# Order of the second layer's matmuls in two-tile expert blocks of an adaLN, attention and mixture-of-experts kernel

## The chip, the cores and the metric

The kernel runs on one core of a Trainium2 chip. The metric is the device time of one execution in microseconds (us), the median of the runs. TensorE is written PE (its weight loads PEld), VectorE is DVE, ScalarE is ACT, GpSimd is POOL, SyncE is SP.

## The reference

The input is 4096 tokens of 256 features. Two residual steps follow each other:

```
h = layernorm(x) * (1 + ca) + sa
x = x + ga * attention(h)          # 16 heads of 64, linear attention
h = layernorm(x) * (1 + cb) + sb
x = x + gb * ffn(h)

gate_probs = softmax(x @ Wg + bg)                 # 8 experts, the top 2 are kept and renormalised
h   = gelu(einsum('bsf,efh->bseh', x, W1) + b1)   # 256 -> 1024
out = einsum('bseh,ehf->bsef', h, W2) + b2        # 1024 -> 256
y   = einsum('bsef,bse->bsf', out, selected)
```

Only the second step's expert part is touched by the change. The kernel computes each token for its two chosen experts alone.

## The kernel before, in words

After attention and routing, the tokens of each expert stand in a list, and the rest of the kernel (from about 405 us of the trace) works through it in *blocks*. A block holds three tiles or two tiles of 128 tokens of one expert. Each expert first runs one or two three-tile blocks (`Fori(0, three)`, L1610) and then its two-tile blocks (`Fori(0, two)`, L1622); the counts come from the data. The experts run in a loop over three pairs, with the last pair written out behind it (`experts`, L391). Even and odd experts use two sets of weight buffers, and the next expert's weights are split in the last engines' spare time of a three-tile block.

fp32 precision is made of three matmuls: each operand is split into a high and a low part, and high*high, high*low, low*high are added (`three_terms`, L369). One block goes through the engines like this:

1. PE, `first` (L1572): 8 slices m of the hidden dimension, 6 matmuls each, 48 in all, into PSUM banks 0 to 3. It starts when DVE has written `xT_lo` (semaphore `s_blo`, L1575). After every second slice it adds one to `s_f1`.
2. ACT, `rows_block` (L811): for each pair of slices k = 0 to 3, waits for `s_f1`, applies the gelu twice into `hid` (L820), then copies the pair to `hid_hi` (L827).
3. DVE, `rows_block` (L1277): for each pair k, waits for ACT and writes `hid_lo` (L1289), which adds one to `s_hid`. Just ahead of pair 3 it does `take(gv + 1)` (L1251): it copies the next block's gate values and normalises the next block's three row tiles in `listed` (L1256, three instructions), which adds one to `s_norm`.
4. PE, `second` (L1591): out of `hid_hi`, `hid_lo` and the expert's `w2`, one accumulation per tile i, in bank 6 + i. It takes a range of slices (`chunks`); 3 matmuls per slice and tile, so 24 per tile and 48 per two-tile block. For tile 0 it waits for `s_hid` before each even slice (L1601); the other tiles use the same slices later and don't wait.
5. In the midst of `second`, PE runs `block_T(gv + 1)` (L1558): it waits for `s_norm` and transposes the next block's rows with 6 instructions (L1563).
6. ACT turns the transposed rows into `xT_full` (L801, two instructions), DVE splits them into `xT_hi` and `xT_lo` (L1247, L1248, two of each); the end of that allows the next block's `first`. POOL's `gather` (L567) also waits for the transposes: it then fetches the rows of the block after the next into `listed` by three indirect DMAs (L576).
7. When a tile's accumulation is complete (`s_f2`), DVE adds the bias and multiplies by the gate (L1299, L1300), and POOL scatters the tile to `out` with an accumulating indirect DMA (L588).

Each engine runs its own stream of instructions in the order in which they are written; semaphores alone tie them together. PE's stream in the two-tile loop is the only thing that the change touches. In the three-tile loop PE's order is: `most` (slices 0 to 5) of tile 0, the transposes, `most` of tile 1, `end` (slices 6 and 7) of tile 0, `most` of tile 2, `end` of tile 1, `end` of tile 2.

Of the kernel before, what the change touches and what calls it, by code (L numbers as in the profile page):

```python
# [26 lines left out]
M = FH // P  # L27
# [56 lines left out]
def adaln_block(nc, x, w_qkv, w_out, b_out, Wg, bg, W1, b1, W2, b2, cvec, wmod, out):  # L84
    ctx = ExitStack()
    with ctx:
# [282 lines left out]
        def three_terms(pairs):  # L369

            ops = [(a, b) for (ah, al), (bh, bl) in pairs for a, b in ((ah, bh), (ah, bl), (al, bh))]
            return [(a, b, i == 0, i == len(ops) - 1) for i, (a, b) in enumerate(ops)]
# [35 lines left out]
        def now(eng, reg):  # L408
            return eng.snap(reg, min_val=0, max_val=MAXB)
# [914 lines left out]
        def _(pe):  # L1324
# [233 lines left out]
            def block_T(n):  # L1558

                pe.wait_ge(s_norm, n + 1)  # L1560
                for c in range(C):
                    for i in range(BI):
                        last = pe.transpose(ps[:, XTB + c, i * P:(i + 1) * P], listed[:, i, c * P:(c + 1) * P], ident[:, :])  # L1563
                last.then_inc(s_bt, 1)
# [5 lines left out]
            def expert(e, par, three, two, last_expert):  # L1570

                def first(gv, size):  # L1572

                    T = size * P
                    pe.wait_ge(s_blo, gv + 1)  # L1575
                    for m in range(M):
                        k = m // 2
                        if m == 0:
                            pe.wait_ge(s_gelu, gv * 4 + FOUR)
                        if size == 3 and m in (4, 6):  # L1580
                            pe.wait_ge(s_gelu, gv * 4 + (k - 1 + FOUR))
                        if m == (3 if size == 3 else 6):
                            pe.wait_ge(s_y, gv * 3 + THREE)
                        to = ps[:, k, (m % 2) * T:(m % 2 + 1) * T] if size == 2 else ps[:, m % 4, 0:T]
                        col = slice(m * P, (m + 1) * P)
                        for w_, a, st, sp_ in three_terms([((w1_hi[par][:, c, col], w1_lo[par][:, c, col]), (xT_hi[:, c, 0:T], xT_lo[:, c, 0:T])) for c in range(C)]):
                            last = pe.matmul(to, w_, a, start=st, stop=sp_)  # L1587
                        if m % 2:
                            last.then_inc(s_f1, 1)

                def second(gv, size, i, chunks):  # L1591

                    bank = Y2 if i == 2 else Y0 + i
                    if 0 in chunks:
                        pe.wait_ge(s_y, gv * 3 + (i + 1))
                        if i == 2:
                            pe.wait_ge(s_gelu, gv * 4 + (M // 2 + FOUR))
                    r = slice(i * P, (i + 1) * P)
                    for m in chunks:
                        if i == 0 and m % 2 == 0:  # L1600
                            pe.wait_ge(s_hid, gv * 4 + (m // 2 + 1 + FOUR))  # L1601
                        for a, w_, st, sp_ in three_terms([((hid_hi[:, m, r], hid_lo[:, m, r]), (w2_hi[par][:, m, :], w2_lo[par][:, m, :]))]):
                            last = pe.matmul(ps[:, bank, 0:D], a, w_, start=m == 0 and st, stop=m == M - 1 and sp_)  # L1603
                    if M - 1 in chunks:
                        last.then_inc(s_f2, 1 if i < size - 1 else BI - i)

                pe.wait_ge(s_wlo, now(pe, w) + 1)
                pe.sem_inc(s_turn_pe, 1)
                most, end = range(0, M - 2), range(M - 2, M)
                with pe.Fori(0, three) as b:  # L1610
                    gv = now(pe, g)
                    first(gv, 3)
                    second(gv, 3, 0, most)
                    block_T(gv + 1)
                    second(gv, 3, 1, most)
                    second(gv, 3, 0, end)
                    second(gv, 3, 2, most)
                    second(gv, 3, 1, end)
                    second(gv, 3, 2, end)
                    pe.reg_add(g, g, 1)  # L1620
                    pe.reg_add(w, w, 1)
                with pe.Fori(0, two) as b:  # L1622
                    gv = now(pe, g)
                    first(gv, 2)
                    for k in range(M // 2):
                        if k == 2:
                            block_T(gv + 1)
                        for i in range(2):
                            second(gv, 2, i, range(2 * k, 2 * k + 2))
                    pe.reg_add(g, g, 1)  # L1630

            experts(pe, g, expert)


# [22 lines left out]
```

## Time and profile before

| what | value |
|---|---|
| three runs | 843.56, 845.4 and 846.81 us, median 845.4 |
| the profiled execution's own time | 845.4 us |
| its span, first to last instruction | 843.7 us |
| mean granted TensorE clock | 0.954 of full speed |
| PE busy | 772.9 us, 92% of the span |
| DVE, ACT, POOL busy | 71%, 55%, 38% |
| chain that ended last, by engine | PE 68%, DVE 18%, issue 7%, ACT 2%, POOL 2% |
| of it PE L1587 (`first`) and PE L1603 (`second`) | 20% and 20% of the span |

The page divides the span into 40 slices of 21 us; the expert blocks fill slices 20 to 40. A timeline row gives start, duration, engine, line, operation, output and inputs, shapes and the count of like instructions merged into it; in brackets stands how long the engine had been idle before it and what released it. Matmuls overlap their neighbours, so a row's duration is longer than the distance to the next row. Start-to-start distances are what counts, and a merged row of six transposes lasts from the first start to the last one's end.

### The profile page before, as it was taken

The numbers are of one execution on the slowest core, as the hardware profiler recorded it, in microseconds if no ns is written. First come the engines' busy times: TensorE is split into PE (matmuls) and PEld (weight loads), VectorE is DVE, ScalarE is ACT, GpSimd is POOL, SyncE is SP. The second block draws the span as 40 slices with busy tenths as digits, with TensorE's granted clock in tenths as the row PEclk, the third lists the DMA queues.
The fourth block names the chain that finished last, engine by engine and source line by source line (L and its number), as shares of the span: only waits on it lengthen the run. The fifth ranks groups of instructions, "written<-read, shape, count | busy, mean of one in ns | idle before, by whom it ended". The sixth has DMA issues, their size and how long they took to land.

```text
span 843.7 us, 17533 instructions
## 1 busy us (share of the span) xinstructions
PE 772.9 (92%) x5848; PEld 703.0 (83%) x5849; DVE 600.2 (71%) x1310; ACT 462.9 (55%) x843; POOL 322.2 (38%) x294
## 2 busy tenths in 40 slices
PE   5989999999998999954699999999999999999992
PEld 4767877888886779854699999999999999999992
DVE  6899999888999425797275755767666686775652
ACT  4565565665644413175365656565475674765461
POOL 2432332232222004001255454646544554546453
PEclk9999999999999999955699999999999999999997
DMA  8400000000001045416144442626325335333332
GB/s 288 144 1 1 2 1 2 2 1 1 2 1 50 2 146 186 141 50 153 59 119 84 107 92 41 153 43 156 56 45 144 57 46 152 49 45 56 54 50 38
DMA packets 45638, 59.56 MB, mean 71 GB/s; under 512 B 8018, under 2 KB 38804, under 8 KB 45460
## 3 DMA queue, kind: packets, MB, share of 16 engines
q0 software_dynamic: 14400, 21.98, 15.0%
q1 hardware_dynamic: 31188, 36.93, 13.7%
q8 instruction: 29, 0.48, 0.2%
q14 instruction: 21, 0.17, 0.1%
HBM read 40.63 MB, written 18.27 MB: 70 GB/s over the span
## 4 chain that ended last, share of the span: by engine, by line
PE 68%; DVE 18%; issue 7%; ACT 2%; POOL 2%; DMA 1%; DVEq 0%; SPq 0%; ACTq 0%; POOLq 0%
PE ps L1587 20%; PE ps L1603 20%; PE ps L1410 7%; PE ps L1368 6%; PE ps L1493 3%; PE ps L1431 3%; PE ps L1563 3%; DVE at_hi L1191 2%; DVE q_max L914 2%; PE ps L1419 2%; DVE q_sum L921 2%; DVE k_blk L1024 2%; PE ps L1513 1%; DVE q_exp L915 1%; DVE listed L1256 1%
## 5 line engine op out<-in xcount | busy, mean ns | idle before, releaser
L820 ACT ACTIVATE hid<-ps,b_col 128x256 f32<-128x256 f32 (+1 forms) x232 | 104.8, 502 | 104.2 <-PE ps L1587 103.2
L1603 PE MATMUL ps<-w_hi,hid_hi 128*128 128x256 f32 x544 | 155.1, 285 | 0.2
L1603 PE MATMUL ps<-w_lo,hid_hi 128*128 128x256 f32 x544 | 151.6, 279 | 0.0
L1603 PE MATMUL ps<-w_hi,hid_lo 128*128 128x256 f32 x544 | 151.6, 279 | 0.0
L1587 PE MATMUL ps<-xT_hi,w_hi 128*128 128x256 f32 (+1 forms) x464 | 143.0, 308 | 5.6 <-DVE xT_lo L1248 2.9
L1289 DVE TENSOR_TENSOR hid_lo<-hid,hid_hi 128x512 fp32r<-128x512 f32 (+1 forms) x116 | 89.7, 783 | 73.2 <-ACT hid_hi L827 56.5
L1587 PE MATMUL ps<-xT_hi,w_lo 128*128 128x256 f32 (+1 forms) x464 | 140.5, 303 | 0.0
L1587 PE MATMUL ps<-xT_lo,w_hi 128*128 128x256 f32 (+1 forms) x464 | 140.5, 303 | 0.0
L588 POOL DMA_INDIRECT out<-y,y_id x68 | 119.5, 1758 | 38.8 <-POOL y_id L583 22.3
L527 POOL TENSOR_TENSOR q_n<-q_exp,q_rec 128x1024 f32<-128x1024 f32 x32 | 61.0, 1905 | 172.4 <-DVE q_rec L922 172.4
L576 POOL DMA_INDIRECT listed<-xrows,gid x93 | 92.1, 990 | 45.2 <-POOL gid L572 26.3
L1603 PEld LDWEIGHTS ps<-w_hi,hid_hi 128*128 128x128 f32 x544 | 102.2, 188 | 1.5 <-DVE hid_lo L1289 1.4
L1603 PEld LDWEIGHTS ps<-w_lo,hid_hi 128*128 128x128 f32 x544 | 102.3, 188 | 0.0
L1603 PEld LDWEIGHTS ps<-w_hi,hid_lo 128*128 128x128 f32 x544 | 102.0, 187 | 0.0
L1587 PEld LDWEIGHTS ps<-xT_hi,w_hi 128*128 128x128 f32 x464 | 88.7, 191 | 10.6 <-issue 8.4
L1368 PE MATMUL ps<-wqk_hi,h_q 128*128 128x512 f32 x248 | 92.4, 415 | 0.4 <-DVE q_exp L915 0.4
L677 ACT ACTIVATE k_exp<-ps,k_new 128x512 f32<-128x512 f32 x64 | 44.1, 689 | 83.0 <-DVE k_new L1025 81.6
L1587 PEld LDWEIGHTS ps<-xT_lo,w_hi 128*128 128x128 f32 x464 | 88.8, 191 | 0.0
L1587 PEld LDWEIGHTS ps<-xT_hi,w_lo 128*128 128x128 f32 x464 | 88.7, 191 | 0.0
L827 ACT ACTIVATE hid_hi<-hid 128x512 fp32r<-128x512 f32 (+1 forms) x116 | 82.0, 707 | 8.6 <-ACT hid L820 5.1
L1410 PE MATMUL ps<-h_q,wqk_hi 128*128 128x512 f32 x256 | 80.7, 396 | 0.0
L801 ACT ACTIVATE xT_full<-ps,modc 128x384 f32<-128x384 f32 x60 | 37.1, 668 | 52.5 <-PE ps L1563 52.2
(209 smaller groups left out, 1462.7 us busy)
## 6 DMA issues: line engine op xcount, KB each, us to landing
w_raw<-in_L_ffn_W SPq DMA_DIRECT2D x16, 1024.0 KB
x_all<-in_L_attn_x SPq DMA_DIRECT2D x8, 512.0 KB, 9.6
out<-x_all SPq DMA_DIRECT2D x8, 512.0 KB, 3.0
xrows<-x_all SPq DMA_DIRECT2D x8, 512.0 KB, 4.7
listed<-xrows,gid POOLq DMA_INDIRECT x93
out<-y,y_id POOLq DMA_INDIRECT x68
wqk_raw<-in_L_attn_w_qkv SPq DMA_DIRECT2D x2, 512.0 KB, 7.1
wqk_raw<-in_L_attn_w_qkv SPq DMA_DIRECT2D x1, 1024.0 KB, 11.4
```

The costliest lines, as they stand in the source:

```text
L527: pool.tensor_tensor(q_n[:, s % 2, i, :].rearrange("p (h d) -> p h d", d=DH), q_exp[:, i % 2, :].rearrange("p (h d) -> p h d", d=DH), bc(q ...
L576: pool.indirect_dma_start(listed[:, i, :], None, xrows[:, :], bass.IndirectOffsetOnAxis(ap=gid[:, i:i + 1], axis=0)).then_inc(s_rows, 16)
L588: pool.indirect_dma_start(out[:, :], bass.IndirectOffsetOnAxis(ap=y_id[:, i:i + 1], axis=0), y[:, i, :], None, compute_op=ALU.add).then_in ...
L677: act.activation(k_exp[:, n % 2, :], ps[:, KT + n % 2, :], ACT.Exp, bias=k_new[:, s % 2, j:j + 1]).then_inc(s_ke, 1)
L801: act.activation(xT_full[:, c, :], ps[:, XTB + c, 0:BT], ACT.Identity, bias=modc[:, 2, c:c + 1], scale=modc[:, 3, c:c + 1]).then_inc(s_bfu ...
L820: ins = act.activation(hid[:, m, 0:T], src, ACT.Gelu_apprx_tanh, bias=b1_col[:, bass.ds(e, 1), m])
L827: act.activation(hid_hi[:, m, 0:T], hid[:, m, 0:T], ACT.Copy).then_inc(s_hidhi, 1)
L1289: dve.tensor_tensor(hid_lo[:, m, 0:T], hid[:, m, 0:T], hid_hi[:, m, 0:T].bitcast(F32), ALU.subtract).then_inc(s_hid, 1)
L1368: last = pe.matmul(ps[:, b + half, :], a, w, start=st, stop=sp_)
L1410: last = pe.matmul(ps[:, KT + n % 2, :], w, a, start=st, stop=sp_)
L1587: last = pe.matmul(to, w_, a, start=st, stop=sp_)
L1603: last = pe.matmul(ps[:, bank, 0:D], a, w_, start=m == 0 and st, stop=m == M - 1 and sp_)
```

## The change: one order of `second` in the two-tile loop is replaced by another

In the two-tile loop, PE went through the slices in four pairs and did both tiles of a pair before the next, with the transposes behind the second pair. Now it goes through slices 0 to 5 of tile 0, the transposes, slices 0 to 5 of tile 1, and then slices 6 and 7 of tile 0 and of tile 1. The number of matmuls, transposes and semaphore waits is unchanged. `most` and `end` are the ranges that the three-tile loop uses.

```
                 with pe.Fori(0, two) as b:
                     gv = now(pe, g)
                     first(gv, 2)
-                    for k in range(M // 2):
-                        if k == 2:
-                            block_T(gv + 1)
-                        for i in range(2):
-                            second(gv, 2, i, range(2 * k, 2 * k + 2))
+                    second(gv, 2, 0, most)
+                    block_T(gv + 1)
+                    second(gv, 2, 1, most)
+                    second(gv, 2, 0, end)
+                    second(gv, 2, 1, end)
                     pe.reg_add(g, g, 1)
```

## Rows read from the trace of the kernel before

**Rows 1.** The page: PE's total, and the granted TensorE clock in 40 slices.

```profile
PE 772.9 (92%) x5848; PEld 703.0 (83%) x5849; DVE 600.2 (71%) x1310; ACT 462.9 (55%) x843; POOL 322.2 (38%) x294
PEclk9999999999999999955699999999999999999997
```

**Rows 2.** Instructions of line L1289: durations in ns, then counts by shape.

```profile
L1289 DVE TENSOR_TENSOR hid_lo<-hid,hid_hi x116: 681/693/990, 417.8 to 824.4; 128x512 fp32r<-128x512 f32 x76, 128x768 fp32r<-128x768 f32 x40
```

**Rows 3.** PE's timeline, a two-tile block behind a two-tile block.

```profile
443.16 0.38 PE L1587 MATMUL ps<-xT_hi,w_hi 128*128 128x256 f32 x1
...
449.02 0.28 PE L1603 MATMUL ps<-w_hi,hid_hi 128*128 128x256 f32 x1
...
451.75 0.82 PE L1563 MATMUL ps<-ident,listed 128*128 128x128 f32 x6
...
455.12 0.28 PE L1603 MATMUL ps<-w_hi,hid_lo 128*128 128x256 f32 x1
455.44 0.43 PE L1587 MATMUL ps<-xT_hi,w_hi 128*128 128x384 f32 x1
```

**Rows 4.** ACT's, DVE's and POOL's timelines in the same block.

```profile
445.32 0.84 ACT L820 ACTIVATE hid<-ps,b_col 128x256 f32<-128x256 f32 x2 [3.58 <-PE ps L1587]
...
449.82 0.69 DVE L1289 TENSOR_TENSOR hid_lo<-hid,hid_hi 128x512 fp32r<-128x512 f32 x1 [0.70 <-ACT hid_hi L827]
...
450.52 1.05 DVE L1256 TENSOR_SCALAR listed<-listed 128x256 f32<-128x256 f32 x3
...
454.74 0.56 DVE L1248 TENSOR_TENSOR xT_lo<-xT_full,xT_hi 128x384 fp32r<-128x384 f32 x1
...
444.21 0.95 POOL L576 DMA_INDIRECT listed<-xrows,gid  x1 [0.30 <-issue]
```

**Rows 5.** Timelines of a two-tile block behind a three-tile block: PE, ACT, DVE.

```profile
430.51 0.28 PE L1603 MATMUL ps<-w_hi,hid_lo 128*128 128x256 f32 x1
430.62 0.28 PE L1587 MATMUL ps<-xT_hi,w_hi 128*128 128x256 f32 x1
...
436.56 0.38 PE L1603 MATMUL ps<-w_hi,hid_hi 128*128 128x256 f32 x1
...
439.49 0.38 PE L1563 MATMUL ps<-ident,listed 128*128 128x128 f32 x2
...
432.46 0.84 ACT L820 ACTIVATE hid<-ps,b_col 128x256 f32<-128x256 f32 x2 [3.76 <-PE ps L1587]
...
435.81 1.90 DVE L1289 TENSOR_TENSOR hid_lo<-hid,hid_hi 128x512 fp32r<-128x512 f32 x3
...
437.71 1.05 DVE L1256 TENSOR_SCALAR listed<-listed 128x256 f32<-128x256 f32 x3
```

**Rows 6.** The same place in the seventh expert: PE's first matmul, DVE's normalisation.

```profile
749.65 0.28 PE L1587 MATMUL ps<-xT_hi,w_hi 128*128 128x256 f32 x1
...
756.57 1.05 DVE L1256 TENSOR_SCALAR listed<-listed 128x256 f32<-128x256 f32 x3
```

**Rows 7.** A three-tile block: DVE's normalisation, then PE before and at the transposes.

```profile
465.21 1.06 DVE L1256 TENSOR_SCALAR listed<-listed 128x256 f32<-128x256 f32 x3
...
465.94 0.28 PE L1603 MATMUL ps<-w_hi,hid_lo 128*128 128x256 f32 x1
466.32 0.87 PE L1563 MATMUL ps<-ident,listed 128*128 128x128 f32 x6
```

**Rows 8.** PE across two changes of expert, and DVE ahead of the second.

```profile
510.20 0.28 PE L1603 MATMUL ps<-w_hi,hid_lo 128*128 128x256 f32 x1
510.93 0.43 PE L1587 MATMUL ps<-xT_hi,w_hi 128*128 128x384 f32 x1 [0.45 <-issue]
...
713.46 0.56 DVE L1248 TENSOR_TENSOR xT_lo<-xT_full,xT_hi 128x384 fp32r<-128x384 f32 x1
...
713.83 0.28 PE L1603 MATMUL ps<-w_hi,hid_lo 128*128 128x256 f32 x1
714.19 0.43 PE L1587 MATMUL ps<-xT_hi,w_hi 128*128 128x384 f32 x1
```

## The prediction

> **What bounds the kernel now.** I read the page first. PE is the busiest engine and its clock is at the full level in every slice behind slice 20, where the expert blocks are [rows 1]. The chain of waits through that half is mostly matmuls of the two expert layers, so a pause of PE there is time. The instructions of line L1289 count the blocks: 76 of the two-tile shape and 40 of the three-tile shape, four per block, so 19 two-tile and 10 three-tile blocks [rows 2]. The change acts in the 19 alone.
>
> Then I laid the timelines of PE, ACT and DVE over one two-tile block and counted from its first matmul at 443.16 [rows 3]. `second` starts at +5.86, the transposes at +8.59, the last matmul at +11.96, the next block's `first` at +12.28. PE's matmuls are 0.12 us apart in `first` (5.86 for 48), and 2.73/24 = 0.114 in `second` ahead of the transposes. Only one place in the block is a pause: 455.12 to 455.44 is 0.32 where a run-on would be 0.12 (as 430.51 to 430.62 is behind a three-tile block [rows 5]). It ends 0.14 after DVE's last `xT_lo` (454.74 + 0.56 = 455.30 [rows 4]): the next block's inputs are late by 0.2 us because only 24 matmuls stand between the transposes and the block's end. That is one margin. The other is at the transposes: DVE ends the normalisation at 450.52 + 1.05 = 451.57, +8.41, and PE gets to them at +8.59, 0.18 later [rows 3, 4]. The two-tile block is tight at both ends of this step, and the change moves it.
>
> **The change part by part.**
>
> *Counts.* The same 48 + 48 matmuls and 6 transposes are issued, with the same waits; nothing is added in busy time.
>
> *The waits for `hid_lo`.* Tile 0 now needs the pairs 6 matmuls apart instead of 12. Pair 2 is needed after 12 matmuls, 12 x 0.114 = 1.37 behind 449.02, at 450.39, and is ready at 449.82 + 0.69 = 450.51 [rows 3, 4]. That would be a stop of 0.15, but it is swallowed by the next one: the transposes behind slices 0 to 5 have to wait longer in any case. Pair 3 isn't needed until after the transposes, when it is long ready.
>
> *The transposes come 6 matmuls earlier,* behind 18 instead of 24. PE would be there at 449.02 + 18 x 0.114 = 451.07, +7.91, and the rows are normalised at +8.41. So they now wait for DVE. The three-tile blocks have this wait already: the normalisation ends at 465.21 + 1.06 = 466.27 and the transposes start 0.05 later, after a last matmul at 465.94 [rows 7]; they then take 0.87 instead of 0.82, so 0.05 more. Queued behind the waiting transposes on PE is all the rest of the block, 30 matmuls, so the wait is on the path.
>
> *Behind the transposes* stand 30 matmuls instead of 24. In the old order transposes and 24 matmuls take 455.12 - 451.75 = 3.37 from the first start to the last. The matmuls of a stream that had a pause are 0.118 apart (the 24 from 436.56 to 439.49, with 0.23 for the first, [rows 5]). So it becomes 3.37 + 6 x 0.118 + 0.05 = 4.13. `xT_lo` follows the transposes by 455.30 - 451.75 = 3.55, plus 0.14 to the first matmul, 3.69 (3.74 with the slower transposes), which is less than 4.13 + 0.12. So the late inputs are covered and the pause of 0.2 at the block's end closes, wherever that alone caused it.
>
> *What closing it brings.* A block that starts without a pause has its hidden values sooner. ACT's first gelu starts 445.32 - 443.16 = 2.16 after the first matmul when PE paused, 432.46 - 430.62 = 1.84 when it ran on [rows 3 to 5]. ACT and DVE then go pair by pair at a fixed pace, so the end of the normalisation moves from +8.41 to about +8.09. The last two experts' blocks come out still earlier: 756.57 + 1.05 - 749.65 = +7.97 [rows 6].
>
> The Trainium skill has a sentence that fits this: "TensorE: Matmul & The Clock Gate", section "Step-by-step: what each phase is for", says that the drain of one matmul is hidden under the next only while they follow without a gap. A gap then costs more than its own length; the 0.32 between the two gelu starts, against 0.2 of pause, points the same way.
>
> *Sum by kind of block* (transposes at the end of the normalisation + 0.05, last matmul 4.13 later, next block 0.12 behind that):
> - Six two-tile blocks behind a three-tile block, with weights being split. DVE is late there and the normalisation ends at 437.71 + 1.05, +8.14; PE after 18 matmuls (one at 0.23, the rest 0.118) is there at +5.94 + 2.24 = +8.18. Transposes at about +8.19, next block at +12.39 to +12.44, before 443.16 - 430.62 = 12.54. They gain 0.12 each, 0.7 us.
> - Two blocks inside an expert: +8.14, last matmul +12.27, next block +12.39 against 12.28: 0.12 each, 0.2 us lost.
> - Seven blocks that end an expert. There the pause stays, since PE's sequencer needs it to read the next expert's counts: 713.83 to 714.19 is 0.36 though `xT_lo` ended at 714.02, and at the pair loop's end 510.20 to 510.93 is 0.73 [rows 8]. What counts is the last matmul: +12.27 instead of +11.96, 0.31 each, six times, 1.9 us. The seventh is in the seventh expert (7.97 + 0.05 + 4.13 = 12.15): 0.2 us.
> - The seventh expert's other three: 12.27 against about 12.26: nothing, 0.05 us together. The kernel's last block: 0.2 us.
>
> Together -0.7 + 0.2 + 1.9 + 0.2 + 0.05 + 0.2 = +1.85 us. The profiled execution took 845.4 us, 1.7 more than its span, and is the median of the three runs, so both give 847.2 us, +0.2%.
>
> *What hides at nothing.* POOL's gather waits for the transposes. They come 0.4 sooner after the block's start, so its DMAs do too; before, its last one is issued by 444.21 + 0.95 = 445.16 and DVE wants the rows at 450.5 [rows 4], so there are over 5 us for the landing. DVE's gate products of tile 0 and 1 still find their sums 6 matmuls apart at the end, as before. If the cover of the gather were gone, the normalisation would be late by as much in each block; nothing in the rows is near that.
>
> **Rivals.**
>
> *A, slower: the normalisation does not move with the pause.* If the gelu's later start (2.16) belongs to following a two-tile block (DVE's products of the last tile, ACT's loop) and not to PE's pause, then 11 blocks keep +8.41, the transposes wait 0.32 longer, and the time is 847.2 + 11 x 0.32 = 850.7 us. For it: in both kinds the block before differs as well as the pause. Against it: in both rows it is PE, and nothing else, that released ACT. It decides if the wait at the transposes is over about 0.35 us in blocks behind two-tile blocks.
>
> *B, faster: the transposes hardly wait.* If ACT and DVE come earlier still, the transposes start at +7.9 in the 13 blocks outside the first kind: 0.24 less each, 3.1 us, so 844.1; if the pause at the change of expert closes too (7 x 0.2), 842.7 us. For it: the normalisation at +7.97 in the seventh expert. Against it: its start is tied to pair 2 of `hid_lo`, and that to ACT's pace; the sequencer's work at a change of expert is seen by itself [rows 8].
>
> *C, much slower: the clock.* The clock row is at full level behind slice 20, and the three-tile blocks have such a wait in each of ten places there. So by this trace the pauses cost no clock. The Trainium skill's "TensorE: Matmul & The Clock Gate", section "A second HAM failure mode: psum-queue depth-cycling", warns that frequent short idle moments between groups of matmuls make the clock fall back again and again. By that rule each of 19 pauses could put the 30 matmuls behind it at half speed, 19 x 3.5 = 67 us more, about 914 us. The trace speaks against it.
>
> **How the numbers follow.** The forecast 847.2 gets 0.62, with its own range 845.2 to 849.2 (each term can be off by 0.1 us in 19 blocks, 2 us). A gets 0.18, B 0.15, C 0.01, and 0.04 is left for what I don't see. From the middle of B (843) to a little above A (851.3) more than 8 in 10 is held. What a measurement of this kernel tells from no change is about 0.5%, 4.2 us: 841.2 to 849.6. Slower by more is A and C, less A's lower part, plus the forecast's upper edge: 0.18. Faster by more needs over twice B's mean: 0.06. The same: 0.76.
>
> **What would show it.** In the changed kernel, 18 matmuls of `second`, then transposes 0.05 behind the end of the normalisation in nearly every two-tile block. The next `first` 0.12 behind the last matmul inside an expert, but 0.3 to 0.7 at a change of expert. ACT's first gelu at +1.84 in all blocks that start without a pause; at +2.16 it is A. A period of 12.4 for two-tile blocks inside an expert, 12.6 for those that end one. DVE waiting for gathered rows, or a lower clock behind slice 20, would make the account wrong altogether.

## The result and the profile after: 7.3 us slower

| | before | after |
|---|---|---|
| median and range of the runs | 845.7 us (843.56 to 846.81), 4 runs | 853.03 us (852.72 to 853.74), 4 runs |
| ratio, with its 95% interval | 1 | 1.0091 (1.0069 to 1.0112) |
| profiled execution, its span | 845.4, 843.7 us | 851.4, 849.6 us |
| mean granted TensorE clock | 0.954 | 0.955 |

The forecast was 847.2 us. The kernel took 853.0, above the forecast's range (849.2) and above the top of rival A's (851.3). The page of the changed kernel shows the same number of PE instructions and, behind slice 20, the same clock row as [rows 1] (the 7 in slice 40 stands behind the last matmuls, in both), so nothing was added and rival C did not happen:

```profile
PE 776.7 (91%) x5848; PEld 704.3 (83%) x5849; DVE 600.9 (71%) x1310; ACT 463.5 (55%) x843; POOL 322.9 (38%) x294
PEclk9999999999999899955799999999999999999997
```

The chain of work that ended last moved, by engine, from PE (68% to 63%) to ACT (2% to 6%):

```profile
PE 63%; DVE 18%; issue 8%; ACT 6%; POOL 1%; DMA 1%; ACTq 1%; SPq 0%; DVEq 0%; POOLq 0%
```

I measured every block's period, from its first matmul to the next block's, in both traces. "Behind" names the block that went before:

| blocks | number | period before | period after | change, sum |
|---|---|---|---|---|
| two-tile behind three-tile | 6 | 12.53 to 12.61 | 12.42 to 12.43 | -0.8 us |
| two-tile behind two-tile, inside an expert | 2 | 12.25, 12.26 | 12.90, 12.95 | +1.35 |
| the same, ending an expert | 6 | 12.27 to 12.68 | 12.63 to 13.61 | +4.8 |
| seventh expert, all four | 4 | 12.23 to 12.27 | 12.29, then 12.84 to 12.85 | +1.8 |
| three-tile | 10 | 17.66 to 20.66 | 17.67 to 20.66 | -0.55 |

The sum is +6.6 us. The spans differ by 5.9, since the kernel's last block (the 19th two-tile block, not in the table) gives 0.7 back: from its first matmul to the end of the program it takes 26.50 us instead of 27.18. Behind PE's last matmul that end is made by POOL, whose last gather and last scatters follow the transposes, and the transposes come 0.57 sooner there. The last scatter of before (its block starts at 816.51) and of after (823.14) start 17.29 and 16.78 us into the block:

```profile
833.80 1.58 POOL L588 DMA_INDIRECT out<-y,y_id  x1 [0.30 <-issue]
...
839.92 1.58 POOL L588 DMA_INDIRECT out<-y,y_id  x1 [0.30 <-issue]
```

The medians differ by 7.3 us and not by 5.9 because the profiled execution of the changed kernel (851.4) was shorter than its four other runs. So 1.3 us of the medians' difference is in no trace.

The first kind did what was forecast. The loss is in the two-tile blocks that stand behind a two-tile block. Here is PE in one of them, to be laid beside [rows 3], and its next block's start:

```profile
442.96 0.28 PE L1603 MATMUL ps<-w_hi,hid_lo 128*128 128x256 f32 x1
443.08 0.28 PE L1587 MATMUL ps<-xT_hi,w_hi 128*128 128x256 f32 x1
...
444.40 0.28 PE L1587 MATMUL ps<-xT_hi,w_lo 128*128 128x256 f32 x1
...
448.84 0.28 PE L1603 MATMUL ps<-w_hi,hid_hi 128*128 128x256 f32 x1
...
450.70 0.38 PE L1603 MATMUL ps<-w_hi,hid_hi 128*128 128x256 f32 x1 [0.28 <-DVE hid_lo L1289]
...
451.76 0.88 PE L1563 MATMUL ps<-ident,listed 128*128 128x128 f32 x6
...
455.88 0.28 PE L1603 MATMUL ps<-w_hi,hid_lo 128*128 128x256 f32 x1
456.24 0.44 PE L1587 MATMUL ps<-xT_hi,w_hi 128*128 128x384 f32 x1
```

The block starts without a pause (442.96 to 443.08, as promised). `first` runs evenly and hands over to `second` at +5.76. But the transposes come at +8.68 where +8.14 was forecast, and behind them everything has the forecast length (451.76 to 455.88 is 4.12, forecast 4.13). The 0.54 comes from ahead of them. ACT, DVE and POOL in the same block, against [rows 4]:

```profile
445.46 0.84 ACT L820 ACTIVATE hid<-ps,b_col 128x256 f32<-128x256 f32 x2 [4.32 <-PE ps L1587]
...
449.95 0.69 DVE L1289 TENSOR_TENSOR hid_lo<-hid,hid_hi 128x512 fp32r<-128x512 f32 x1 [0.70 <-ACT hid_hi L827]
...
450.65 1.05 DVE L1256 TENSOR_SCALAR listed<-listed 128x256 f32<-128x256 f32 x3
...
457.45 0.42 DVE L1299 TENSOR_TENSOR y<-ps,b_bc 128x256 f32<-128x256 f32 x1 [0.80 <-PE ps L1603]
...
440.98 1.04 POOL L576 DMA_INDIRECT listed<-xrows,gid  x1 [0.84 <-POOL gid L572]
442.32 0.98 POOL L576 DMA_INDIRECT listed<-xrows,gid  x1 [0.31 <-issue]
443.61 0.95 POOL L576 DMA_INDIRECT listed<-xrows,gid  x1 [0.30 <-issue]
```

The first gelu starts at 445.46, +2.38. Behind a three-tile block it is +1.84 in both kernels, with the same 12 matmuls of PE ahead of it at the same pace. ACT had been idle for 4.32 us, and PE's 12th matmul had started at 444.40, +1.32 in both kinds. The gelu follows it by 1.06 here and by 0.51 behind a three-tile block. So the matmuls started on time and the semaphore count that follows them (`s_f1`) came about 0.54 late; the trace's own times of the counts say the same, 0.84 behind the 12th matmul's start instead of 0.29. (The trace models when a matmul ends, so it can't tell a late count from a result that was itself late.) From there ACT and DVE keep their old pace: the normalisation ends at 450.65 + 1.05 = 451.70, +8.62, and PE goes on 0.06 later. The last tile's count (`s_f2`) is late in the same way: its last matmul is at 455.88, and DVE's product of it starts at 457.45 after an idle of 0.80 put down to PE.

Of the eleven blocks behind a two-tile block one is an exception: the block that starts at 706.48 had its gelu at +1.84, its transposes at +8.13 and a period of 12.63 where 12.6 was forecast. The three others in the same place (with a like change of expert behind them) took 13.13 to 13.15. So the loss that was not forecast is in the ten blocks with a late count.

The waits of the two kernels over the expert blocks (window from 426 us; us in total, times, longest). After:

```profile
ACT hid L820 <- PE ps L1587: 108.2, 27, 6.5
...
DVE y L1299 <- PE ps L1603: 19.6, 27, 1.9
PEld ps L1603 <- DVE hid_lo L1289: 6.2, 16, 0.6
PEld ps L1563 <- DVE listed L1256: 5.7, 22, 0.3
```

The two last rows are PE's waits for DVE (the profile books them on its weight loads): 6.2 us for `hid_lo` and 5.7 us at the transposes. In the kernel before they were 1.4 and 2.4 us, so PE waits 8.1 us longer in them. The wait that is the cause isn't to be seen as one: it hides among the 108.2 us of ACT's, most of which (the long ones behind a block's last gelu) cost nothing.

### The profile page after: what moved, and what is told of

Its sections match the earlier page's. It is cut to its first block, busy times and chain, and to the rows that moved or that the text cites. A ratio compares the mean times of both kernels' runs of the same rounds, so it can differ in the third digit from the quotient of the medians.

```text
span 849.6 us, 17533 instructions
## 1 busy us (share of the span) xinstructions
PE 776.7 (91%) x5848; PEld 704.3 (83%) x5849; DVE 600.9 (71%) x1310; ACT 463.5 (55%) x843; POOL 322.9 (38%) x294
## 4 chain that ended last, share of the span: by engine, by line
PE 63%; DVE 18%; issue 8%; ACT 6%; POOL 1%; DMA 1%; ACTq 1%; SPq 0%; DVEq 0%; POOLq 0%
PE ps L1603 18%; PE ps L1587 17%; PE ps L1410 7%; PE ps L1368 6%; ACT hid L820 4%; PE ps L1493 3%; PE ps L1563 3%; PE ps L1431 3%; DVE at_hi L1191 2%; DVE listed L1256 2%; DVE q_max L914 2%; PE ps L1419 2%; DVE q_sum L921 2%; DVE k_blk L1024 2%; ACT hid_hi L827 2%
## 5 line engine op out<-in xcount | busy, mean ns | idle before, releaser
L820 ACT ACTIVATE hid<-ps,b_col 128x256 f32<-128x256 f32 (+1 forms) x232 | 104.7, 503 | 113.9 <-PE ps L1587 108.2
L1289 DVE TENSOR_TENSOR hid_lo<-hid,hid_hi 128x512 fp32r<-128x512 f32 (+1 forms) x116 | 89.6, 782 | 71.4 <-ACT hid_hi L827 69.7
L588 POOL DMA_INDIRECT out<-y,y_id x68 | 120.4, 1770 | 38.8 <-POOL y_id L583 14.9
L576 POOL DMA_INDIRECT listed<-xrows,gid x93 | 91.7, 986 | 45.5 <-POOL gid L572 26.2
```

The source lines that it names most:

```text
L576: pool.indirect_dma_start(listed[:, i, :], None, xrows[:, :], bass.IndirectOffsetOnAxis(ap=gid[:, i:i + 1], axis=0)).then_inc(s_rows, 16)
L588: pool.indirect_dma_start(out[:, :], bass.IndirectOffsetOnAxis(ap=y_id[:, i:i + 1], axis=0), y[:, i, :], None, compute_op=ALU.add).then_in ...
L820: ins = act.activation(hid[:, m, 0:T], src, ACT.Gelu_apprx_tanh, bias=b1_col[:, bass.ds(e, 1), m])
L1289: dve.tensor_tensor(hid_lo[:, m, 0:T], hid[:, m, 0:T], hid_hi[:, m, 0:T].bitcast(F32), ALU.subtract).then_inc(s_hid, 1)
```

## The experiments

I went back over the trace of before with this: the gelu at +2.16 in [rows 4] is late by 0.32 too. I had put that down to PE's pause. One more row of the same block shows that this was wrong:

```profile
444.58 0.28 PE L1587 MATMUL ps<-xT_hi,w_lo 128*128 128x256 f32 x1
```

It is the 12th matmul, +1.42. The pause has put it 0.1 later than the +1.32 of a block without one. The gelu then follows it by 0.74 and not by 0.51, and this 0.23 is not PE's pace.

Counts of PE were then compared with the start of the gather, POOL's three indirect DMAs (L576, 1.3 us apart). In both kernels a count is late only if it is due 2.3 to 4.4 us after the first of the three starts, though not each one that is due then is late. Some of the late ones come 3.5 to 3.6 us behind that start, the others 4.2 to 4.4. The old order's first count falls into the first of these windows, the new order's into the second, since its transposes release POOL 0.5 us sooner. That gave a theory G (the gather holds the count) against a theory P (something in the new order of PE, or in its place of the transposes alone).

The chips differ in this, as the second group showed, so each group names its chip's time of the kernel before. That kernel has a trace of its own on the third chip alone.

### First group: one chip, kernel before at 846.04 us (9 runs)

**The gather moved behind the counts.** The new order, and POOL also waits until the running block's last accumulation is complete. Its gather then starts 1.55 us into the next block instead of 2.1 us ahead of it:

```
-            def gather(col, n):
+            def gather(col, n, gv=None):
+                if gv is not None:
+                    pool.wait_ge(s_f2, gv * 3 + (3 + THREE))
...
-                    gather(ahead(b + 2), gv + 2)
+                    gather(ahead(b + 2), gv + 2, gv)
...
-                    gather(ahead(three + b + 2), gv + 2)
+                    gather(ahead(three + b + 2), gv + 2, gv)
```

> New order; POOL's gather also waits for the block's last matmul of the second layer, so its three indirect DMAs start about 3.8 us later. Theory G (PE's count for the first two slices, which ACT waits for, comes late while POOL issues the gather): the first gelu comes back from about 2.4 us to 1.85 us after the block's first matmul in two-tile blocks behind two-tile blocks, their period from about 12.9 to 12.4 us, and the time from 853 to about 847 to 848 us. Theory P (the lateness belongs to PE starting a block behind a two-tile block, wherever the gather is): no change, 853 us.

Measured: 908.08 us, ratio 1.0745 (1.0720 to 1.0769). Both totals were far off, and for a reason that neither theory had: the rows then land too late behind a three-tile block. There DVE waits for them, the normalisation starts up to 12.6 us into the block, and the period is 18.5 to 20.3 us in six blocks. PE stood 4.5 to 5.8 us ahead of the transposes of these six, and its granted clock fell behind the pause, which it does in before and after only behind PE's last matmul: in the first of them it is 1.00 while PE works (428.75 to 437), 0.50, the lower of the two levels, from 442.5 to 447, and 1.00 again from 448. So waits of 5 us cost clock in this kernel, and those of 0.3 us in the changed kernel don't. The blocks behind two-tile blocks still answer the question. ACT and POOL in the one that starts at 500.53:

```profile
502.36 0.84 ACT L822 ACTIVATE hid<-ps,b_col 128x256 f32<-128x256 f32 x2 [5.22 <-PE ps L1589]
...
503.94 0.82 ACT L822 ACTIVATE hid<-ps,b_col 128x256 f32<-128x256 f32 x2
...
505.88 0.84 ACT L822 ACTIVATE hid<-ps,b_col 128x256 f32<-128x256 f32 x2 [0.46 <-PE ps L1589]
...
502.07 1.04 POOL L578 DMA_INDIRECT listed<-xrows,gid  x1 [0.85 <-POOL gid L574]
503.42 0.98 POOL L578 DMA_INDIRECT listed<-xrows,gid  x1 [0.30 <-issue]
504.70 0.95 POOL L578 DMA_INDIRECT listed<-xrows,gid  x1 [0.30 <-issue]
```

The first gelu is on time, 502.36 - 500.53 = 1.83. It is now the third pair that is late: at the pace of 1.39 it would have started at 505.33, and it starts at 505.88, 3.81 us behind the gather's first instruction. So the lateness went with the gather (in others of these blocks by up to 1.3 us), and P has nothing that explains this.

**The same in the old order.** The edit is the one above without the new order.

> Old order with the same later gather. Theory G: the first gelu moves from 2.16 to about 1.85 us, but the old order's period of 12.26 us is bound by PE's matmuls and by the late inputs at the block's end, so the time stays at about 845.5 us. Theory P: nothing moves at all, the gelu stays at 2.16 us.

Measured: 897.1 us, 1.0594 (1.0563 to 1.0625), with the same picture: first gelu on time, normalisation late and periods of up to 20 us behind three-tile blocks. It adds only that the new order isn't needed for either.

**New tile order, transposes behind 24 matmuls.**

```
                     second(gv, 2, 0, most)
+                    second(gv, 2, 1, range(0, 2))
                     block_T(gv + 1)
-                    second(gv, 2, 1, most)
+                    second(gv, 2, 1, range(2, M - 2))
```

> New order with the transposes put back to where they were, behind 24 matmuls (slices 0 to 5 of tile 0, slices 0 and 1 of tile 1). If the place of the transposes is the cause, 845.7 us within 1.5; if the order of the tiles (pair 2 wanted 6 matmuls sooner) is, 850 us or more.

Measured: 849.41 us, 1.0042 (1.0028 to 1.0056), between the two answers that had been written down. The gather starts at -1.59 again as in the kernel before, and the gelu is late by 0.35 to 0.41 only (0.1 of it the pause's). The transposes come at +8.85 to +9.01, for another reason than in the changed kernel. PE and DVE in the block that starts at 486.95:

```profile
486.95 0.38 PE L1587 MATMUL ps<-xT_hi,w_hi 128*128 128x256 f32 x1
...
495.88 0.82 PE L1563 MATMUL ps<-ident,listed 128*128 128x128 f32 x6
...
493.66 0.69 DVE L1289 TENSOR_TENSOR hid_lo<-hid,hid_hi 128x512 fp32r<-128x512 f32 x1 [0.70 <-ACT hid_hi L827]
494.36 1.05 DVE L1256 TENSOR_SCALAR listed<-listed 128x256 f32<-128x256 f32 x3
```

The normalisation ended at 495.41, so it wasn't waited for. Pair 2 of `hid_lo` was ready at 494.35, +7.40, and PE wanted it at +7.2, after 12 matmuls; 12 more matmuls follow it ahead of the transposes. So the early wait for `hid_lo`, which I had called swallowed, costs once other matmuls stand between it and the transposes: 0.36 us at 495.88 against +8.57 in the old order. The late count has a part in this too: in the kernel before on the third chip, where no count is late, pair 2 is ready at +7.10, ahead of the +7.2. This order was not run on such a chip.

**Old pair order, transposes behind 18 matmuls.**

```
                     for k in range(M // 2):
-                        if k == 2:
-                            block_T(gv + 1)
                         for i in range(2):
+                            if k == 1 and i == 1:
+                                block_T(gv + 1)
                             second(gv, 2, i, range(2 * k, 2 * k + 2))
```

> Old order of pairs with the transposes alone moved up by 6 matmuls, behind 18. If the place of the transposes is the cause, about 853 us as the change itself; if the order of the tiles is, about 846 us.

Measured: 853.87 us, 1.0090 (1.0072 to 1.0107): the changed kernel's time, without its tile order. PE, ACT and DVE in the block that starts at 487.78:

```profile
487.78 0.28 PE L1587 MATMUL ps<-xT_hi,w_hi 128*128 128x256 f32 x1
...
496.56 0.87 PE L1563 MATMUL ps<-ident,listed 128*128 128x128 f32 x6 [0.73 <-DVE listed L1256]
...
490.27 0.84 ACT L820 ACTIVATE hid<-ps,b_col 128x256 f32<-128x256 f32 x2 [4.43 <-PE ps L1587]
...
495.45 1.05 DVE L1256 TENSOR_SCALAR listed<-listed 128x256 f32<-128x256 f32 x3
```

Gelu at +2.49, normalisation ended at +8.72, transposes at +8.78, as late as in the changed kernel or a little later. So the place of the transposes is enough for the whole loss. The tile order alone costs 3.4 us on this chip (new_t24), by its early wait for `hid_lo`, but nothing on top: with the transposes behind 18 matmuls both orders take the same time (1.0091 and 1.0090 of the kernel before).

### Second group: another chip, kernel before at 844.23 us (25 runs)

**Plain DMAs for the gather.** The shortest way to ask whether the indirect DMAs hold the count:

```
                 for i in range(BI):
-                    pool.indirect_dma_start(listed[:, i, :], None, xrows[:, :],
-                                            bass.IndirectOffsetOnAxis(ap=gid[:, i:i + 1], axis=0)).then_inc(s_rows, 16)
+                    pool.dma_start(listed[:, i, :], xrows[i * P:(i + 1) * P, :]).then_inc(s_rows, 16)
```

With the new order:

> New order; the gather's three indirect DMAs per block are replaced by three plain DMAs of the same size from fixed rows (so the rows of the expert blocks are not the listed ones, all else is computed as before). Theory G-issue (PE's counts are held while POOL makes the indirect DMAs' descriptors): no late gelu, 1.85 us in all blocks that start without a pause, period 12.4 us, the new order within 1 us of 1.9 us over its counterpart in the old order. Theory G-data (the rows landing in SBUF hold them): the gelu is still late by about 0.5 us, at a shifted time, and the new order still costs 5 us or more over its counterpart.

Measured: 844.21 us, 1.0002 (0.9992 to 1.0011). With the old order:

> Old order with the same plain DMAs in the gather, the counterpart of the kernel before. Both theories: 845 us within 2, since the old order's blocks are bound by PE and by the late inputs at the end, not by the gelu. Theory G-issue: first gelu at 1.85 us plus what PE's own pause takes; G-data: 2.16 us or so as before.

Measured: 843.18 us, 0.9985 (0.9973 to 0.9996). In the first of them all gelus are on time, and the periods are 12.37 to 12.39 inside an expert, 12.59 to 12.62 at its end (13.00 at the end of the pair loop's body) and 12.28 in the seventh expert. That would be G's case, but on this chip there are no late counts with the real gather either (old_early_take below, the old order with the real gather, has its gelus at +1.93), so this group can't say that the plain DMAs did it.

**The normalisation taken earlier.** If the transposes wait for DVE, DVE can do the normalisation ahead of pair 2 instead of pair 3:

```
                     for k in range(M // 2):
-                        if k == M // 2 - 1:
+                        if k == M // 2 - 2:
                             take(gv + 1)
```

With the pair order and the transposes behind 18 matmuls:

> Old order of pairs, transposes behind 18 matmuls, and DVE's normalisation of the next rows one pair sooner (ahead of pair 2 instead of pair 3). If the transposes' wait for the normalisation is all that the new place costs, that wait is gone even with a late gelu (normalisation over at about 7.6 us, PE there at 7.9), the inputs are no longer late, two-tile blocks take about 12.1 us, and the time is about 842 to 843 us, below both kernels. If the lateness strikes elsewhere (pair 2's hid_lo), 846 us or more.

Measured: 837.56 us, 0.9930 (0.9913 to 0.9948). In the kernel before, with nothing else changed:

> Kernel before with the early normalisation alone, transposes behind 24 matmuls. Nothing waits for the normalisation there in two-tile blocks; three-tile blocks lose their wait of 0.3 us at the transposes but want pair 2 about as much later. 845 to 846 us; if it is much below, the gain of the kernel with both is not the transposes' place.

Measured: 842.47 us, 0.9981 (0.9972 to 0.9991). Both are faster than was expected. In the second, the three-tile blocks go from 17.84 (kernel before, third chip) to about 17.58 and the two-tile blocks keep 12.26 inside an expert: their transposes have their place behind 24 matmuls, and the earlier rows are of no use. So 1.8 of the 6.7 us that both edits bring together come from the normalisation alone, in the three-tile blocks. The 842 to 843 that were expected for the first counted the two-tile blocks only. Its twin on the third chip (t18_early_take2), against the kernel before there, gains 2.6 us in the three-tile blocks, 1.5 in the two-tile blocks behind them, 1.9 in the other two-tile blocks and 0.7 in the last block. In the first, the normalisation ends at +6.69, the transposes at +7.80 wait for nothing, 30 matmuls cover what DVE does for the next block, and the period is 12.00.

### Third group: a third chip, kernel before at 844.5 us (25 runs)

The changed kernel without any edit, and beside it the kernel before without any edit:

> The changed kernel once more, unaltered, beside the kernel with the plain DMAs. Theory G-issue (the indirect DMAs hold PE's counts, wherever it runs): 7 us over the kernel before, gelu at about 2.4 us. Theory C (it is the chip on which it ran: the two calls before this one fell on different chips, and the plain-DMA runs and the early-normalisation runs, without any late count, were all of the second call): on a chip without late counts the changed kernel is only 1 to 2 us over the kernel before, with gelus at 1.85 us.

> The kernel before, unaltered, for its profile in this call. G-issue: first gelu at 2.16 us in blocks behind two-tile blocks. C on a chip without late counts: 1.95 us or less. Same time in both, 844 to 846 us.

Measured: 845.52 us (843.64 to 846.5, 10 runs), 1.0012 (1.0002 to 1.0021), and 844.36 us, 0.9998 (0.9988 to 1.0008). On this chip the changed kernel is slower by 0.1%. PE, ACT and DVE of it, in the same block as in the trace after above:

```profile
440.92 0.28 PE L1587 MATMUL ps<-xT_hi,w_hi 128*128 128x256 f32 x1
...
449.05 0.88 PE L1563 MATMUL ps<-ident,listed 128*128 128x128 f32 x6
...
453.53 0.44 PE L1587 MATMUL ps<-xT_hi,w_hi 128*128 128x384 f32 x1
...
442.76 0.84 ACT L820 ACTIVATE hid<-ps,b_col 128x256 f32<-128x256 f32 x2 [3.77 <-PE ps L1587]
...
447.94 1.05 DVE L1256 TENSOR_SCALAR listed<-listed 128x256 f32<-128x256 f32 x3
```

The gelu is at +1.84, the normalisation ends at +8.07, the transposes are at +8.13, and the period is 12.61: step by step what the forecast said. The kernel before on the same chip, in the same block, PE and ACT:

```profile
443.56 0.38 PE L1587 MATMUL ps<-xT_hi,w_hi 128*128 128x256 f32 x1
...
445.49 0.84 ACT L820 ACTIVATE hid<-ps,b_col 128x256 f32<-128x256 f32 x2 [3.34 <-PE ps L1587]
```

It has PE's pause, and its gelu is at +1.93, not at +2.16. So the pause makes the gelu 0.09 later in the block, and does so through the matmuls: the second one starts 0.22 behind the first instead of 0.12. The other 0.23 of the 0.32 in [rows 4] was the late count.

The two best ideas again, on this chip:

> The same kernel as t18_early_take. It was 6.7 us under the kernel before in the second call. If late counts come back here, its transposes still find the rows normalised (7.6 against 7.9 us) and it stays 5 us or more below the kernel before; if the gain needs counts on time, less than 3 us.

> The same kernel as new_direct (new order, plain DMAs from fixed rows in place of the indirect gather). G-issue: on time counts here too and 5 us or more under new_again. C: no difference to new_again beyond 1 us, with or without late counts in both.

Measured: 838.75 us, 0.9929 (0.9912 to 0.9946), and 843.96 us, 0.9998 (0.9988 to 1.0008). The second isn't told apart from the kernel before. Its median is 1.6 us below that of the changed kernel with its real gather, though neither has late counts here; in the old order (second group) it was 1.05 us. The traces show where the plain DMAs save this: in the kernel's last block, which POOL ends. It takes 25.24 us there against 26.68 with the real gather, since POOL issues three plain DMAs in 1.75 us instead of 3.6; all other blocks together differ by 0.15 us.

### Fourth group: a chip with late counts, kernel before at 845.43 us (13 runs)

Still open was whether the chip alone makes the difference, and whether plain DMAs take the late counts away where there are some.

> The changed kernel a third time, unaltered, in a further call. Theory C (late counts belong to the chip, or to the state in which a call finds it): either again 7 us over the kernel before with gelus at about 2.4 us, or again about 1 us over it with gelus at 1.85 us, and nothing in between.

> New order with plain DMAs in place of the indirect gather (expert rows are fixed ones). If this call has late counts in new_third: with plain DMAs they are gone (the gather's indirect DMAs make them) or still there (it is the chip's, whatever the DMA). Without late counts in new_third it tells nothing more: 0.5 us below it.

Measured: 852.33 us (850.8 to 853.21), 1.0068 (1.0047 to 1.0089), and 844.03 us, 0.9973 (0.9961 to 0.9984). The changed kernel is slow again: the difference goes with the chip. Each chip was measured at one time only, so a lasting property of the chip isn't told apart from a state that it was in. With plain DMAs the kernel is 8.3 us faster on the same chip. First the changed kernel, ACT and DVE in the block that starts at 486.55:

```profile
489.04 0.84 ACT L820 ACTIVATE hid<-ps,b_col 128x256 f32<-128x256 f32 x2 [4.43 <-PE ps L1587]
...
494.23 1.05 DVE L1256 TENSOR_SCALAR listed<-listed 128x256 f32<-128x256 f32 x3
```

Then the kernel with plain DMAs in the same block, which starts at 485.73; PE, ACT, DVE and POOL (its lines are one lower):

```profile
485.73 0.28 PE L1586 MATMUL ps<-xT_hi,w_hi 128*128 128x256 f32 x1
...
493.86 0.88 PE L1562 MATMUL ps<-ident,listed 128*128 128x128 f32 x6
...
498.11 0.28 PE L1586 MATMUL ps<-xT_hi,w_hi 128*128 128x256 f32 x1
...
487.57 0.84 ACT L819 ACTIVATE hid<-ps,b_col 128x256 f32<-128x256 f32 x2 [3.77 <-PE ps L1586]
...
492.76 1.05 DVE L1255 TENSOR_SCALAR listed<-listed 128x256 f32<-128x256 f32 x3
...
483.42 1.75 POOL L576 DMA_DIRECT2D listed<-xrows  x3 [0.63 <-POOL gid L572]
```

Gelu at +2.49 in the one and at +1.84 in the other; period 13.05 and 12.38. Block by block the sum of the difference is 7.6 us, 7.5 of it in the two-tile blocks behind two-tile blocks; another 1.3 us is the last block's, as on the third chip, and has nothing to do with late counts. So both are needed: the indirect gather, and a chip that does this.

The rows' own transfer is not what holds the count. With plain DMAs 0.41 MB moves on POOL's queue between 486.0 and 487.5 us, and the first pair's count is due in the midst of it, at 487.34, and is on time. But POOL has issued all three by 485.17. Whether it matters that the DMAs are indirect, or only that POOL issues indirect ones for 3.6 us instead of 1.75, isn't told apart.

> Old order of pairs with the transposes behind 18 matmuls, once more. It was 7.8 us over the kernel before in the call that had late counts. In a call without them, where the normalisation is over at 8.08 us, it costs what the place of the transposes alone costs: 1 to 2 us over the kernel before.

Measured: 853.27 us, 1.0088 (1.0069 to 1.0107), 7.8 us over the kernel before as in the first group.

> The better version again. If this call has late counts: its rows are normalised at about 7.6 us (7.2 and the 0.5 of lateness) and PE is there at 7.9, so it stays 5 us or more below the kernel before. Without late counts: 6 us below, as twice before.

Measured: 836.68 us, 0.9895 (0.9872 to 0.9917). PE, ACT and DVE in the block that starts at 482.81:

```profile
482.81 0.28 PE L1587 MATMUL ps<-xT_hi,w_hi 128*128 128x256 f32 x1
...
490.61 0.82 PE L1563 MATMUL ps<-ident,listed 128*128 128x128 f32 x6
...
494.80 0.29 PE L1587 MATMUL ps<-xT_hi,w_hi 128*128 128x256 f32 x1
...
485.42 0.84 ACT L820 ACTIVATE hid<-ps,b_col 128x256 f32<-128x256 f32 x2 [4.42 <-PE ps L1587]
...
489.22 1.05 DVE L1256 TENSOR_SCALAR listed<-listed 128x256 f32<-128x256 f32 x3
```

The count is held here as well, longer than in the changed kernel: gelu at +2.61, 0.77 late. But the normalisation ends at 490.27, +7.46, ahead of PE's +7.80. The block takes 11.99, like the block of the same kernel on the second chip with its count on time (12.00). So the late count costs nothing here, and this is the fastest kernel of the study: on all three chips it was below the kernel before, by 0.7%, 0.7% and 1.05%. This confirms the cause from the other side: once the transposes no longer wait for the normalisation, the late count is harmless.

## Why the prediction was wrong

**What bounds the kernel now: right.** PE's matmuls, the two tight places and their margins are in the traces as described. Only "full level in every slice behind slice 20" is loose: slice 40 has a 7, behind PE's last matmul.

**The waits for `hid_lo`: right.** A stop of 0.28 stands at 450.70 and is swallowed by the next wait. The new_t24 kernel shows the condition: it isn't swallowed once 12 matmuls and not 6 follow it ahead of the transposes, since PE then comes to them behind the end of the normalisation.

**The transposes wait for the normalisation: right,** 0.05 to 0.06 behind its end in every two-tile block of the changed kernel.

**30 matmuls behind, 4.13 us: right,** 4.12. **The pause at the block's end closes: right,** 0.12 in every block inside an expert, and 0.33 to 0.74 where the expert changes, except from the seventh expert to the last, where it closed too. The row that I took for PE's sequencer, 714.19, was no evidence for it: it stands 0.17 behind `xT_lo`, like any block with late inputs. The changed kernel is: at 456.24 PE starts 0.36 behind its last matmul though `xT_lo` had ended at 455.36.

**What closing it brings: this step failed.** It put all of the gelu's 0.32 down to PE's pause. 0.09 of it was the pause's (kernel before, third chip), the rest was a count of PE's that came late, and it could be seen in the trace that I had: the gelu 0.74 behind the 12th matmul instead of 0.51. The closed pause was to bring the normalisation to +8.09. In the trace of the changed kernel the count is then later still, by 0.54 instead of 0.23, and the normalisation ends at +8.62. In the old order the same lateness had a cover: with the transposes at +8.59, a normalisation that ended at +8.41 cost nothing. The change took the cover away, and by the earlier gather it made the lateness larger. Against the same ten blocks on the third chip that is 0.53 to 0.62 each, 5.7 us together. The block at 706.48 lost nothing. In the traces the change cost 5.9 us where 1.85 was forecast: 5.7 more by the late counts, 0.9 less in the kernel's last block, 0.55 less in the three-tile blocks and 0.2 less in the rest. That the median of 853.0 is 5.8 above the forecast, nearly the same as 5.7, is chance: 4.2 of it is in the profiled execution, and 1.6 is the distance from there to the median.

The Trainium skill's sentence in "TensorE: Matmul & The Clock Gate", section "Step-by-step: what each phase is for", was my support for this step. The runs show that a gap of 0.2 costs the gelu 0.09, and these are in the starts of the matmuls already (0.22 between the first two instead of 0.12). Behind the 12th matmul the gelu comes after 0.51 with the pause and without it. So no run here shows a drain that the gap laid open, and the sentence did not support the step.

**Sum by kind: right where no count is late, but for the last block.** Against the kernel before on the third chip the kinds gave -0.62, +0.25, +1.92 and about +0.1, so 1.6 us, where the forecast had -0.7, +0.2, +1.9 and +0.25, the last block left out. The medians differed by 1.0 us there. The term "+0.2" for the seventh expert's end did not come, since its pause closed. The three-tile blocks gained 0.55 us between the first two traces, which the sum did not have: theirs was a late count too (0.4 to 0.45 us in five of them in the kernel before), due 4.0 us behind the gather's start; with the gather started sooner it is due 4.7 us behind it and on time. And the last block's term had the wrong sign: +0.2 was put down because PE ends later there, but POOL ends the kernel, behind transposes that come sooner: -0.7 between the first two traces and -0.35 on the third chip.

**What hides at nothing: half right.** The rows that POOL fetches did land in time. I asked of the moved gather only whether its data come in time, not what else its start touches.

**Rival A: right that it isn't the pause, with the wrong cause and the wrong price.** "The normalisation does not move with the pause" is what the trace shows. But the cause that A named, DVE's products or ACT's loop behind a two-tile block, isn't it: on the third chip, behind the same two-tile blocks, the gelu is at +1.84. The transposes start 0.8 later than the +7.88 at which PE would come without waits; that is over A's 0.35, though the stop at `hid_lo` takes the first part of it and no wait at the transposes alone is over 0.3. A gave 0.32 for each of 11 blocks, since it took the gelu's place to be fixed at +2.16; it was +2.31 to +2.44 in ten of them. A with 0.54 in place of 0.32 would give 853.1, which is luck again: it has a block too many and the last block's term wrong. Rival B had nothing: no transposes came at +7.9, on any chip, until the normalisation itself was moved. Rival C's rule, the Trainium skill's "A second HAM failure mode: psum-queue depth-cycling" in the same page, was not seen either: 22 waits of up to 0.3 us at the transposes, and the clock at 0.955 against 0.954. The waits of 4.5 to 5.8 us in new_gather_late did lower it.

## What to carry to other kernels

When a consumer starts later than its producer's matmuls allow, work out from a block that is on time when it should have started, and ask for the cause of the whole difference: a margin that covers an unexplained lateness isn't free to be spent. If a step of the bound engine is to come earlier, first move what it waits for: early transposes alone cost 7.8 us on two chips, and together with a normalisation ahead of pair 2 they brought 5.7 to 8.8 us on three. And one chip's margins aren't another's, so a gain of under 1% that rests on 0.2 us margins should be timed on more than one.

## What the hardware did that I had not expected

PE's semaphore counts can come late while its matmuls start on time, when they are due 2.1 to 4.4 us behind the first of three indirect gathers on POOL: `s_f1` by 0.23 to 0.8 us, by up to 1.5 with the moved gather, and the last tile's `s_f2` by 1.2 to 1.5. They then come at one of two moments, 3.5 to 3.6 or 4.2 to 4.5 us behind that start, the first of which is about the end of POOL's third instruction. Not each count that is due in this time is late: `s_f2`, due 2.3 us behind the start, was late in the seven blocks of the changed kernel that end an expert and on time in the others. The scatters (L588, indirect as well) showed nothing like it. Two of the four chips of the experiments had it, as had the first two traces (first gelu late by 0.32 to 0.4 in the old order, its pause's 0.09 included, and by 0.5 to 0.6 in the new; 0.65 to 0.7 on the fourth chip). The other two did not (0.00 in the new order, 0.09 in the old, its pause's), and with plain DMAs it was gone on the fourth chip. Why a count is late, why only on some chips, and why the block at 706.48 (whose third gather started 0.4 later than usual) escaped, stays open; the gather was not tried with fewer or wider instructions, nor plain DMAs that keep POOL busy as long.
